# The later part of a perceiver layer on one core: gate's weights split by halves, regrouped comparisons, a second buffer for the kept features, stacked last features and a reordered tail

## The reference, cut to what matters

```python
# x: 16 x 64 x 1024, context: 16 x 1601 x 256; 1024 tokens in all
x = x + xattn(layernorm(x), ctx, ctx, mask)          # 32 heads, 8 key heads of 32
z = layernorm(x)
s = silu(z @ w_gate.T)                               # 2752 features
_, idx = top_k(-abs(s), 1376)                        # the smaller half in size
s[rows, idx] = 0.0                                   # is dropped, token by token
x = x + (s * (z @ w_up.T)) @ w_down.T
z = layernorm(x)
w = two largest of softmax(z @ router_w.T + router_b), scaled to sum 1
x = x + sum over experts of w * ((z @ A.T) @ Bm.T) * 0.5
```

## Time and profile before

| | us |
|---|---|
| median of 3 runs | 1414.36 (1413.8 to 1415.15) |
| the profiled execution | 1412.86 |
| its span, first to last instruction | 1410.9 |
| mean granted PE clock | 0.988 |
| PE busy (share of the span) | 1362.0 (97%) |
| DVE busy | 981.2 (70%) |
| ACT busy | 739.2 (52%) |
| POOL busy | 929.2 (66%) |

### The profile page before, as it was taken

How to read it: one execution, slowest core, us unless ns; L and a number is a source line. 1 busy time by engine, 2 the same in 40 slices (tenths; PEclk the granted TensorE clock), 3 DMA queues, 4 the chain that set the end, 5 groups by cost and what they waited for, 6 DMA issues and landing times.

```text
span 1410.9 us, 30485 instructions
## 1 busy us (share of the span) xinstructions
PE 1362.0 (97%) x12727; PEld 1014.1 (72%) x12727; DVE 981.2 (70%) x1324; ACT 739.2 (52%) x935; POOL 929.2 (66%) x613
## 2 busy tenths in 40 slices
PE   4999999999999999899999999999997999999996
PEld 4555555555555555599999998888886888887874
DVE  6888888888888888870001899989898223255654
ACT  6788888888888888732224625243331111111211
POOL 0899888888888888813443343223233899999881
PEclk9999999999999999999999999999998999999998
DMA  9023323233333330024337348384736876855561
GB/s 357 33 104 102 136 97 114 99 117 104 117 98 121 100 107 18 16 77 169 139 124 299 122 164 276 126 294 126 275 104 244 299 258 189 272 186 181 160 202 45
DMA packets 110016, 217.62 MB, mean 154 GB/s; under 512 B 7200, under 2 KB 82864, under 8 KB 104880
## 3 DMA queue, kind: packets, MB, share of 16 engines
q1 hardware_dynamic: 88928, 192.89, 39.4%
q10 hardware_dynamic: 20944, 22.70, 5.1%
HBM read 173.63 MB, written 41.94 MB: 153 GB/s over the span
## 4 chain that ended last, share of the span: by engine, by line
PE 77%; DVE 13%; DMA 4%; ACT 3%; issue 2%; POOL 0%; DVEq 0%; ACTq 0%; SPq 0%
PE fast_psum L1896 16%; PE fast_psum L2033 16%; PE fast_psum L1914 15%; PE fast_psum L1981 14%; PE fast_psum L1933 6%; DVE fast_below L1392 4%; PE fast_psum L2003 2%; DMA fast_mag<-s 1%; PE fast_psum L1940 1%; PE fast_psum L2017 1%; PE fast_psum L2063 1%; DMA sk<-fast_sx 1%; PE fast_psum L2084 1%; PE fast_psum L1919 1%; DVE fast_near L1429 1%
## 5 line engine op out<-in xcount | busy, mean ns | idle before, releaser
L1322 DVE TENSOR_TENSOR fast_masked<-fast_psum,fast_mask_t 128x1024 f32<-128x1024 f32 (+1 forms) x416 | 488.2, 1218 | 72.0 <-PE fast_psum L1896 70.4
L1178 POOL TENSOR_TENSOR fast_pair<-fast_probs 128x1024 f32<-128x1024 f32 x192 | 457.0, 2383 | 96.1 <-PE fast_psum L1933 47.9
L1659 ACT ACTIVATE fast_probs<-fast_masked 128x1024 f32<-128x1024 f32 (+1 forms) x416 | 437.8, 1058 | 68.0 <-DVE fast_masked L1322 52.8
L1896 PE MATMUL fast_psum<-fast_qT,fast_kraw 32*128 32x256 f32 (+1 forms) x3328 | 245.7, 401 | 6.5 <-issue 3.3
L1914 PE MATMUL fast_psum<-fast_probs,fast_vraw 128*32 128x256 f32 (+1 forms) x3328 | 226.5, 386 | 0.8 <-ACT fast_probs L1659 0.8
L1896 PEld LDWEIGHTS fast_psum<-fast_qT,fast_kraw 32*128 32x128 f32 (+1 forms) x3328 | 152.9, 181 | 92.6 <-DVE fast_masked L1322 54.0
L1233 POOL TENSOR_TENSOR fast_d_lo<-fast_d_raw,fast_d_hi 128x256 fp32r<-128x256 f32 (+1 forms) x264 | 198.2, 781 | 5.3
L1209 POOL TENSOR_TENSOR fast_g_lo<-fast_g_raw,fast_g_hi 128x2816 fp32r<-128x2816 f32 x14 | 87.8, 6274 | 145.5 <-ACT fast_g_hi L1718 123.4
L1981 PE MATMUL fast_psum<-fast_g_hi,fast_z_hi 128*128 128x352 f32 x512 | 166.4, 325 | 1.8 <-POOL fast_g_lo L1209 1.8
L1981 PE MATMUL fast_psum<-fast_g_hi,fast_z_lo 128*128 128x352 f32 x512 | 165.5, 323 | 0.0
L1981 PE MATMUL fast_psum<-fast_g_lo,fast_z_hi 128*128 128x352 f32 x512 | 165.0, 322 | 0.0
(11 more groups left out here) (164 smaller groups left out, 1898.2 us busy)
## 6 DMA issues: line engine op xcount, KB each, us to landing
fast_d_raw<-w_down SPq DMA_DIRECT2D x63, 512.0 KB, 3.7
fast_kraw<-ctx_t SPq DMA_DIRECT2D x32, 800.5 KB, 6.0
fast_vraw<-ctx_nat SPq DMA_DIRECT2D x16, 1536.0 KB
fast_g_raw<-w_gate_up SPq DMA_DIRECT2D x15, 1408.0 KB, 7.3
fast_mag<-s SPq DMA_DIRECT2D x8, 1376.0 KB, 9.8
fast_sx<-s SPq DMA_DIRECT2D x8, 1376.0 KB, 6.8
sk<-fast_sx SPq DMA_DIRECT2D x8, 1376.0 KB, 7.1
fast_u_raw<-w_up_t SPq DMA_DIRECT2D x21, 512.0 KB, 5.4
```

What stands on the lines that cost most here:

```text
L1178: pool.tensor_tensor(pair[:, n % PAIR_BUFS], both[:, :, 0, :], both[:, :, 1, :], ALU.add).then_inc(paired, 1)
L1322: dve.tensor_tensor(into, of, m, ALU.add).then_inc(mask_added, 1)
L1659: act.activation(probs[0:r, g % RING, hp * HALF:(hp + 1) * HALF], masked[0:r, h % SLOTS, :], ACT.Exp).then_inc(exp_done, 1)
L1896: last = pe.matmul(scores[0:r, (2 * g + hp) % SLOTS, h % 2, i * 256:(i + 1) * 256], kraw[b % BUFS][q, u, c * P:c * P + r], qT[q, b, u, :], ...
```

## The change

- Gate: the copy to the high part and the subtraction for the low part are made in two halves of four `k` each, for each load after the first; PE waits for the second half ahead of its fifth `k` of the pass's first tile.
- Search: pair 1's first three comparisons stand together after the last gate slot, the rest in groups of up to three at later slots of up.
- A second `sx` buffer lies where gate's second raw weights lay, and tile 7 uses a buffer of `mag`. Each `sx` has its own semaphores. SP's order in up is new.
- ACT issues the first loads of `sk` and `u_t` after slot 34 instead of 40, and waits there for six stored tiles instead of three.
- Step 21 of each group: its 64 features are loaded twice, so that 128 rows hold them stacked; the weights are loaded twice too, POOL puts the low part into the lower 64 rows of `d_hi`. Two pairs of matmuls take the place of three.
- Tail: three last steps (`HELD`) instead of two do tile 6 ahead of tile 7; the last step finishes a half at a time, and DVE adds and takes statistics a half at a time; the Exp table is asked for ahead of `take_zt(7)`; mixing, its adds and the last store go by halves.
- The slab's alignment is 128 instead of 512 bytes, and its start may move by that.

```diff
--- before.py
+++ after.py
@@ -727,7 +732,7 @@
         OUT = H_LO + HS * TW
-        LINE = 512
+        LINE = 128
         sb("slab", [P, SLAB + LINE // 4], F32)
...
@@ -770,7 +775,8 @@
         below = [at(f"below{j}", WIDE + 3 * I + I // 2 * j, [I], BF16)[:, :] for j in range(2)]
-        sx = at("sx", WIDE + 4 * I, [I])[:, :]
+        sx_of = [at(f"sx{j}", start, [I])[:, :] for j, start in enumerate((WIDE + 4 * I, THIN + 2 * HT * GJ))]
+        sx = [sx_of[t % 2] for t in range(TILES - 1)] + [mag[(TILES - 3) % MAGS]]
         t_sk = [at(f"t_sk{j}", THIN + 3 * BW * j, [3, BW]) for j in range(2)] + [
...
@@ -854,6 +861,13 @@
         steps = [0]
+        g_split = lambda n, h=1: 1 if n == 0 else 2 * n + h
+        HELD = DS
+        twice = lambda n: n % IC == UF
+
+        def loads(n, ring, every=IC):
+
+            return sum(2 if m % every == every - 1 else 1 for m in range(n % ring, n + 1, ring))
...
@@ -939,13 +953,15 @@
         GATE_COUNT_AT = {42: (0, 0), 44: (0, 1), 45: (0, 2), 46: (0, 3), 48: (0, 4), 49: (0, 5)}
-        UP_ABS_AT = {6: 4, 12: 5, 19: 6, 25: 7}
-        UP_COUNT_AT = {0: (1, 0), 1: (1, 1), 2: (1, 2), 3: (1, 3), 4: (1, 4), 5: (1, 5),
-                       13: (2, 0), 14: (2, 1), 15: (2, 2), 16: (2, 3), 17: (2, 4), 18: (2, 5),
-                       26: (3, 0), 27: (3, 1), 28: (3, 2), 29: (3, 3), 30: (3, 4), 31: (3, 5)}
+        GATE_COUNTS = {63: (1, (0, 1, 2))}
+        UP_ABS_AT = {7: 4, 12: 5, 21: 6, 26: 7}
+        UP_COUNT_AT = {1: (1, (3, 4)), 4: (1, (5,)),
+                       14: (2, (0, 1, 2)), 16: (2, (3, 4)), 19: (2, (5,)),
+                       28: (3, (0, 1, 2)), 30: (3, (3, 4)), 33: (3, (5,))}
         GATE_MAG_AT = {9: 2}
-        UP_SK_AT = {1: 1, 5: 2, 7: 3, 12: 4, 13: 5, 18: 6}
-        UP_MAG_AT = {0: 4, 5: 5, 7: 6, 12: 7}
+        UP_SK_AT = {1: 1, 6: 2, 8: 3, 13: 4, 15: 5, 19: 6}
+        UP_SX_AT = {0: 2, 2: 3, 7: 4, 9: 5, 14: 6, 15: 7}
+        UP_MAG_AT = {0: 4, 6: 5, 8: 6, 13: 7}
         LOAD_X_AT = {0: 0, 12: 1, 30: 2}
...
@@ -1046,19 +1062,27 @@
             def load_sx(t):
-                if t >= 1:
-                    sp.wait_ge(sk_stored, 16 * t)
-                sp.dma_start(sx, s[t * P:(t + 1) * P, :]).then_inc(sx_full, 16)
+                if t == 1:
+                    sp.wait_ge(g_lo_done, g_split(LOADS - 1))
+                elif t == TILES - 1:
+                    sp.wait_ge(kept, t - 1)
+                elif t >= 2:
+                    sp.wait_ge(sk_stored[t % 2], 16 * (t // 2))
+                sp.dma_start(sx[t], s[t * P:(t + 1) * P, :]).then_inc(sx_full[t % 2], 16)
...
                 sp.wait_ge(kept, t + 1)
-                sp.dma_start(sk[t * P:(t + 1) * P, :], sx).then_inc(sk_stored, 16)
+                if t == TILES - 1:
+                    sp.wait_ge(sk_stored[t % 2], 16 * (t // 2))
+                sp.dma_start(sk[t * P:(t + 1) * P, :], sx[t]).then_inc(sk_stored[t % 2], 16)
...
                 sp.dma_start(d_raw[n % DS][0:rows(k), :], w_down[k * P:k * P + rows(k), :]).then_inc(d_full[n % DS], 16)
+                if twice(n):
+                    sp.dma_start(d_raw[n % DS][UREST:P, :], w_down[UF * P:I, :]).then_inc(d_full[n % DS], 16)
...
@@ -1107,9 +1137,9 @@
                 if p + 1 == PASSES:
+                    load_sx(1)
                     store_sk(0)
                     load_mag(3)
-                    load_sx(1)
                 store_gate(p)
...
@@ -1122,12 +1152,12 @@
                         sp.wait_ge(s_stored[j], 16 * NCH)
+                if f in UP_MAG_AT:
+                    load_mag(UP_MAG_AT[f])
+                if f in UP_SX_AT:
+                    load_sx(UP_SX_AT[f])
                 if f in UP_SK_AT:
                     store_sk(UP_SK_AT[f])
-                    if UP_SK_AT[f] + 1 < TILES:
-                        load_sx(UP_SK_AT[f] + 1)
-                if f in UP_MAG_AT:
-                    load_mag(UP_MAG_AT[f])
                 if f == UF - 2:
...
@@ -1205,9 +1235,11 @@
                     pool.wait_ge(pv_done, ASTEPS)
-                pool.wait_ge(g_hi_done, n + 1)
-                pool.tensor_tensor(g_lo[j][:, :, :], g_raw[raw(n)][:, :, :], g_hi[j][:, :, :].bitcast(F32),
-                                   ALU.subtract).then_inc(g_lo_done, 1)
+                for h in range(2):
+                    ks = slice(4 * h, 4 * h + 4)
+                    pool.wait_ge(g_hi_done, g_split(n, h))
+                    pool.tensor_tensor(g_lo[j][:, ks, :], g_raw[raw(n)][:, ks, :], g_hi[j][:, ks, :].bitcast(F32),
+                                       ALU.subtract).then_inc(g_lo_done, 1)
...
@@ -1220,17 +1252,20 @@
             for n in range(STEPS):
-                j, r = n % DS, rows(n % IC)
-                pool.wait_ge(d_full[j], 16 * (n // DS + 1))
+                j = n % DS
+                rs, low = (slice(UREST, P), d_hi[j]) if twice(n) else (slice(0, P), d_lo[j])
+                pool.wait_ge(d_full[j], 16 * loads(n, DS))
                 if n >= DS:
...
                     pool.wait_ge(u_done, 2 * UF)
-                pool.tensor_copy(d_hi[j][0:r, :], d_raw[j][0:r, :]).then_inc(d_hi_done, 1)
+                if n % IC == 0 and n >= 1:
+                    pool.wait_ge(d_lo_done, n)
+                pool.tensor_copy(d_hi[j][:, :], d_raw[j][:, :]).then_inc(d_hi_done, 1)
                 pool.wait_ge(d_hi_done, n + 1)
...
                     qs = slice(q * 256, (q + 1) * 256)
-                    last = pool.tensor_tensor(d_lo[j][0:r, qs], d_raw[j][0:r, qs], d_hi[j][0:r, qs].bitcast(F32),
+                    last = pool.tensor_tensor(low[rs, qs], d_raw[j][rs, qs], d_hi[j][rs, qs].bitcast(F32),
                                               ALU.subtract)
...
@@ -1515,10 +1550,24 @@
+            def add_in_by_halves(i):
+                t = GROUPS[2][i]
+                dve.wait_ge(xin_full, 16 * TILES)
+                for o in range(2):
+                    os = slice(o * 512, (o + 1) * 512)
+                    dve.wait_ge(half_done, 2 * i + o + 1)
+                    dve.tensor_tensor(xin[t][:, os], bank[2 * i + o][:, :], xin[t][:, os], ALU.add).then_inc(added, 1)
+                    dve.wait_ge(added, 2 * t + o + 1)
+                    last = dve.bn_stats(ln3.stats[:, o, :], xin[t][:, os])
+                last.then_inc(ln3.steps_done, 1)
+
             def normalise3(t):
...
                     dve.wait_ge(z3_turned, 2 * (t - ZS + 1))
+                if t >= 6:
+                    ln3.vector_rest(dve, xin[t][:, :], z3[t % ZS][:, :], t, 1.0, z3_ready)
+                    return
                 ln3.vector(dve, xin[t][:, :], z3[t % ZS][:, :], t, 1.0, z3_ready)
...
@@ -1715,7 +1763,9 @@
                     act.wait_ge(g_done, n * HT)
-                act.copy(g_hi[n % 2][:, :, :], g_raw[raw(n)][:, :, :]).then_inc(g_hi_done, 1)
+                for h in range(2):
+                    ks = slice(4 * h, 4 * h + 4)
+                    act.copy(g_hi[n % 2][:, ks, :], g_raw[raw(n)][:, ks, :]).then_inc(g_hi_done, 1)
...
@@ -1754,17 +1804,27 @@
                     compare(*GATE_COUNT_AT[q])
+                if q in GATE_COUNTS:
+                    p, rounds = GATE_COUNTS[q]
+                    for r in rounds:
+                        compare(p, r)
...
                 if b == 0:
-                    act.wait_ge(sk_stored, 16 * (GROUPS[gi][-1] + 1))
+                    stored = max(GROUPS[gi][-1] + 1, TILES - 2)
+                    for j in range(2):
+                        act.wait_ge(sk_stored[j], 16 * ((stored + 1 - j) // 2))
                 if q >= BLOCKS:
...
                               ).then_inc(sk_full[q % BLOCKS], 16)
+                if b == GB - 1:
+                    act.dma_start(t_sk[q % BLOCKS][:, 0:m, w:BW],
+                                  sk[t0 * P:(t0 + m) * P, UF * P:I].rearrange("(t p) c -> p t c", p=P)
+                                  ).then_inc(sk_full[q % BLOCKS], 16)
...
@@ -1787,8 +1847,10 @@
                 if i in UP_COUNT_AT:
-                    compare(*UP_COUNT_AT[i])
-                if i == 2 * UF - 2:
+                    p, rounds = UP_COUNT_AT[i]
+                    for r in rounds:
+                        compare(p, r)
+                if i == 2 * UF - 8:
                     for q in range(2):
...
@@ -1838,6 +1901,7 @@
             ln3.scalar(act, 7)
+            act.activation(first_exp[:, :], ones[:, 0:1], ACT.Exp)
             take_zt(7)
...
@@ -1977,6 +2041,8 @@
                 for k in range(DK):
+                    if i == 0 and n >= 1 and k == 4:
+                        pe.wait_ge(g_lo_done, g_split(n, 1))
                     for a, (zp, wp) in enumerate(((z_hi, g_hi), (z_hi, g_lo), (z_lo, g_hi))):
...
@@ -2010,17 +2076,16 @@
                 q, c = n // 2, n % 2 * P
-                pe.wait_ge(sk_full[q % BLOCKS], 16 * (q // BLOCKS + 1))
+                pe.wait_ge(sk_full[q % BLOCKS], 16 * loads(q, BLOCKS, GB))
                 if n >= 2:
...
                 for i in range(len(GROUPS[gi])):
```

(29 more changed lines are left out.)

58 lines of the change are left out of this document (34 added, 24 removed).

## The result

| | us, median (lowest to highest, runs) | ratio to before, 95% interval |
|---|---|---|
| before | 1414.45 (1412.97 to 1417.05, 10) | |
| after | 1407.66 (1402.94 to 1413.52, 10) | 0.9945 (0.9923 to 0.9967) |

That is 7.8 us less by the ratio, between 4.7 and 10.9, where 12.0 were forecast. 1407.66 lies just inside the range of 1398 to 1408. The runs of the changed kernel spread over 10.6 us, those of the kernel before over 4.1.

The account below looks back on a forecast made before the run. TensorE was taken as the bound nearly everywhere. Terms: -8.0 (gate and hand-over), 0 (clock), -1.37 -0.43 (stacking), +0.4 (DMA), -2.6 (tail) = -12.0 us, from the median 1414.36 to 1402.4; range 1398 to 1408.

Parts of the forecast that it names:

- rivals A: Hand-over: DVE takes the DMA wait's place; search gains nothing, DVE ends at 1084.98; 1406.7 us; chance 0.14.
- Rival B: Down's first data come late as before: 5.6 us of stall in steps 2 to 4; 1407.6 us; chance 0.12.
- both of its own signs: Prediction is wrong if PE waits on u_out or u_lo in up, or if DVE ends search after 1084.
- Gate's halves: Late gate passes: both PE waits for g_lo (0.95, 0.86 us) go; PE leaves gate 1.8 us earlier.
- The search, free at 1080.7: Search beside up: DVE free at about 1080.7; down starts 8.0 us earlier, gate's 1.8 among them.
- Up, costed at nothing: Up stage: a stalled round can break the 0.8 us cover at q=63 by a microsecond or two; counted as nothing.
- rival C: Up stage: grouped comparisons starve PE, which waits for u_copied and u's weights; 1424 us; chance 0.04.
- PE's own path at the hand-over: Up to down with DVE free in time: PE's own steps start down at 1081.4, 9.3 us earlier.
- The clock: First down matmuls: shorter idle time gains 1.65 us or ends 1.25 worse than now; taken as 0.
- Stacking: Step 21 of each group: one of three matmul pairs goes; 1.37 us in group 0, 0.43 counted in group 1.
- Early down weights: First down steps: weights wanted 8 us earlier; cost between nothing and 5.6 us, taken as 0.4.
- The tail: After 1380 us: gain of 1.6 us with the slow clock, 3.65 if the clock stays up; taken as 2.6.

Follow-up runs that it names:

- one_slot_mag_first: Changed kernel with ACT's comparisons one per slot as before, and mag(3) loaded ahead of sx(1) in the last gate pass: 1405.92 us, ratio 0.9948.
- held2: Changed kernel with two held steps of tile 7 (HELD = 2) instead of three: 1408.69 us, ratio 0.9950.
- no_u_low: Changed kernel with GpSimd's subtraction for u_lo cut to one column and PE using u_hi instead, as many matmuls: 1404.76 us, ratio 0.9929.
- full_rows: late_keep with the stacked step's and last step's second product, and DVE's low part, on all 128 rows: 1400.06 us, ratio 0.9891.
- late_keep: Changed kernel with mag(3) loaded ahead of sx(1), and tile 7's choose and keep moved into the down projection: 1399.90 us, ratio 0.9904.
- unstacked: Changed kernel with step 21 of each group as before (64 rows), the features still loaded twice: 1407.48 us, ratio 0.9952.
- before_gate_line: Kernel before with only gate's weights in halves and the slab aligned to 128 bytes instead of 512: 1413.46 us, ratio 0.9984.
- gate_whole: Changed kernel with gate's weights split in one piece again on ACT and GpSimd, one wait on PE: 1409.78 us, ratio 0.9958.
- late_guess: Changed kernel with mag(3) loaded ahead of sx(1), and a DVE instruction of about 0.9 us put ahead of pair 1: 1410.35 us, ratio 0.9960.

## Why the prediction was right in the time and wrong in a step

The time lay 0.3 us inside the upper end of the range. That end was set by rivals A and B, not by the forecast's own path, so the hit owes more to the width of the range than to the working. By both of its own signs the prediction was wrong: PE waited for u_out and u_lo in up, and DVE ended the search at 1088.1, after 1084.

- **Gate's halves**, 1.8: measured 1.8 to up's first matmul. That nothing behind it may hold PE at its old time was said, and it was the case here too.
- **The search, free at 1080.7**: this is the step that failed. DVE was free at 1088.1. The wait of 11.58 us for a load went, and DVE's waits fell by 6.8 us, but its stalls beside GpSimd rose by 14.1. Pair 3 was to start at 1007.8, bound by ACT's 29th copy; it started at 1012.0, bound by DVE itself, which was still at pair 2. Its last round was to begin at 1040.7 and began at 1049.35. The rest was to take 40.0 us and took 38.8. The reading of the kernel before was wrong too: the 41.9 us behind that round held 5.4 us of stalls and waits, not 2. The row of 2.37 us was in the prediction, as something that happens now and then; the stalls should have been summed (24.8 us before), and it should have been asked what sets them. In the kernel before, pair 1 had only 4.2 us of them, with its rounds 5.44 us apart like PE's blocks; one_slot_mag_first brought such rounds back, with 5.0. Rival A, DVE in the place of the DMA wait, is what happened, but for 7.3 us and not 4.3: the search did not stay where it was, it ended 3.1 us later. It had a chance of 0.14.
- **Up, costed at nothing**: PE waited three times, 1.95 us by the rows and 2.8 with what each costs around it. This is rival C in small. The cover of 0.8 us at q=63 was named as the thin one; the wait for u_out came at 883.52, behind the next group, and in held2 at 873.07 too, the fifth block.
- **PE's own path at the hand-over**, 2.9: 2.2 to 2.4 us where DVE was free (no_u_low, full_rows, late_keep).
- **The clock**, 0 between -1.65 and +1.25: 0.86 and 0.80 granted in the two 10 us from 1080 on, and the first step of down takes 7.32 us against 7.19 before: no gain. It stays up for the first 10 us only with the short idle times of late_keep, full_rows and no_u_low.
- **Stacking**, 1.37 and 0.43: mis-sized. 0.54 in group 0 (4.74 to 4.20 us); the 0.53 of group 1 came before the wait at the router, which stayed (1.86 us). The groups got 1.7 us shorter all the same, because each of some 40 other steps takes 4.447 instead of 4.475 us, 1.1 in all. Its cause stays open: it isn't the stacking (4.447 in unstacked too), nor the slab's place (4.475 in before_gate_line).
- **Early down weights**, 0.4: nothing in the changed kernel, where down started late; 1.8 and 4.7 us of waits where it started at 1080.9, 2.4 where it started at 1082.8 (late_keep, no_u_low, full_rows). Rival B would have had that, had A not come first.
- **The tail**, 2.6: 3.7, and 0.5 more behind it. Router 6 took 2.12 us: the case of 3.65. Part of this is luck of the clock. The old tail took 28.4 us in the kernel before and 27.1 in before_gate_line, the new one 24.4 to 24.6 in six traces and 26.0 in four, so the gain lies between 1.1 and 3.9 us, depending on which two executions are compared.

The forecast fell 5.3 us short in the median. In the trace 7.3 of it are missing at the first down matmul and 1.6 come back in the tail and behind it. That the hand-over hung on DVE was shown by late_keep: with tile 7 out of the way it shrank to 2.4 us, and the time to 1399.9.

## What to carry to other kernels

When a wait of an engine goes, sum first what that engine loses to its neighbours now, instruction by instruction, over the whole stretch: a wait can be the room in which such losses were hidden. Two engines that run in step with a third can fall into good or bad places by tenths of a microsecond, and a wide spread of run times can be a sign of it. Look for the last step on the path that the next stage does not need yet; moving it (here the keeping of a tile that only group 2 reads) was worth more than making its engine faster (1399.9 us against 1404.8 in no_u_low).

## What the runs showed of the hardware

- A change between matmuls of 128 and of 64 rows costs 0.20 us (pairs 0.66 apart instead of 0.46). The Trainium skill, page TensorEngine Tiling (Array Packing), Key Properties, says that TensorE drains when its tiling mode changes; this trace agrees, if 64 rows count as another mode.
- In the up stage, DVE's small steps with two inputs, and its TENSOR_SCALAR on 2 or 8 columns, stand still for the rest of a GpSimd instruction (up to 2.4 us). TENSOR_SCALAR on one column and the one-input count of 3.08 us never do (448 such counts in 14 traces). GpSimd's cast stands in the same way behind a long two-input step of DVE (3.61 us instead of 1.04). In the changed kernel and its variants: 8.2 us of stalls without 21 of GpSimd's subtractions, 33 to 40 with them; 25 in the kernel before.
- After an idle time of 1.82 to 1.87 us at the router the granted clock fell in six traces (0.83 in 10 us in gate_whole, 1.7 to 2.3 us lost) and stayed up in seven (there router 0 took 2.12 us). In the tail, after an idle time near 1.1 us, the same stretch from the last transposes took 24.4 to 24.6 us in six traces and 25.97 to 26.03 in four.
- PE's waits cost more than the idle time in their rows: 1.95 us in three rows made up 2.8 us longer in the changed kernel, 0.57 us in one row 0.8 in late_guess.
